# Token stage and routing stage merged into one block, with the tile order of the token stage rearranged

## The reference, cut to what matters

```python
x = L0_attn_x                                   # (4, 1024, 256): 4096 tokens of 256
x = layernorm(x + attention(x, kernel, WO))     # 16 heads of 64
probs = softmax(x @ gate_W)                     # 8 experts
topk_w, topk_idx = top_k(probs, 2)              # and topk_w normalized
out = 0.5 * gelu(x @ shared_W + shared_b)
for e in range(8):
    out = out + combine[:, e] * (gelu(x @ W1[e] + b1[e]) @ W2[e] + b2[e])
x = layernorm(x + layernorm(out) * gamma + beta)
```

## Time and profile before

| | us |
|---|---|
| median of 3 runs | 1883.01 (1877.25 to 1883.25) |
| the profiled execution, its own time | 1879.8 |
| its span | 1878.0 |
| TensorE busy | 1757.6 (94%) |
| VectorE busy | 1385.4 (74%) |
| ScalarE busy | 1046.4 (56%) |
| GpSimd busy | 353.7 (19%) |

### The profile page before, as it was taken

How to read it: one execution, slowest core, us unless ns; L and a number is a source line. 1 busy time by engine, 2 the same in 40 slices (tenths; PEclk the granted TensorE clock), 3 DMA queues, 4 the chain that set the end, 5 groups by cost and what they waited for, 6 DMA issues and landing times. The chain is left out here.

```text
span 1878.0 us, 31867 instructions
## 1 busy us (share of the span) xinstructions
PE 1757.6 (94%) x10909; PEld 1193.3 (64%) x10909; DVE 1385.4 (74%) x2213; ACT 1046.4 (56%) x1554; POOL 353.7 (19%) x399
## 2 busy tenths in 40 slices
PE   6999999999999999999999997987659999999986
PEld 5555555555555555555555553877549999999982
DVE  5888888888888888888888887555566655566647
ACT  5555555565555555555655654544455544455537
POOL 1000000000000000000000000011127766666654
PEclk9999999999999999999999998998879999999998
DMA  5011111111111111311111112444123333233335
GB/s 173 29 46 35 35 46 35 35 41 40 34 35 45 36 35 40 127 34 40 40 35 40 40 35 86 146 157 157 55 91 90 88 80 77 59 87 89 87 49 178
DMA packets 80198, 127.09 MB, mean 68 GB/s; under 512 B 12753, under 2 KB 46737, under 8 KB 77777
## 3 DMA queue, kind: packets, MB, share of 16 engines
q1 hardware_dynamic: 61808, 98.27, 15.6%
q0 software_dynamic: 18272, 27.31, 7.3%
HBM read 86.72 MB, written 38.83 MB: 67 GB/s over the span
## 5 line engine op out<-in xcount | busy, mean ns | idle before, releaser
L450 ACT ACTIVATE a_e<-banks 128x1024 f32<-128x1024 f32 x512 | 490.4, 1026 | 334.9 <-PE banks L346 334.9
L559 DVE TENSOR_TENSOR a_esum<-a_esum,a_e 128x1024 f32<-128x1024 f32 x384 | 470.4, 1225 | 80.5 <-ACT a_e L450 52.9
L360 PE MATMUL banks<-a_e,a_v 128*64 128x512 f32 x2048 | 481.6, 602 | 0.0
L360 PEld LDWEIGHTS banks<-a_e,a_v 128*64 128x64 f32 x2048 | 130.0, 136 | 251.2 <-issue 227.6
L346 PE MATMUL banks<-a_qh,a_kh 64*128 64x512 f32 x1024 | 222.8, 432 | 5.3 <-issue 5.3
L63 POOL MEMSET ident<- 128x128 f32 x1 | 0.2, 204 | 1139.9 <-POOLq L112 1139.9
L346 PEld LDWEIGHTS banks<-a_qh,a_kh 64*128 64x128 f32 x1024 | 96.2, 184 | 173.4 <-issue 107.9
L346 PE MATMUL banks<-a_qh,a_kl 64*128 64x512 f32 x1024 | 202.4, 391 | 0.0
L1790 ACT ACTIVATE e_g<-banks,e_b1c 128x256 f32<-128x256 f32 x280 | 114.9, 471 | 154.1 <-PE banks L1737 152.9
L346 PE MATMUL banks<-a_ql,a_kh 64*128 64x512 f32 x1024 | 200.2, 388 | 0.0
L1750 PE MATMUL banks<-e_w2h,e_hh 128*128 128x256 f32 x560 | 162.3, 290 | 4.5 <-issue 1.9
(11 more groups left out here) (232 smaller groups left out, 3294.4 us busy)
## 6 DMA issues: line engine op xcount, KB each, us to landing
attn_out<-a_ot SPq DMA_DIRECT2D x64, 256.0 KB, 2.0
a_inv<-inv_rows SPq DMA_DIRECT2D x126, 128.0 KB, 2.9
a_w<-w_qkv SPq DMA_DIRECT2D x32, 256.0 KB, 3.1
raw<-attn_out SPq DMA_DIRECT2D x4, 2048.0 KB, 8.8
t_ot<-attn_out SPq DMA_DIRECT2D x4, 2048.0 KB, 8.2
raw<-w_up SPq DMA_DIRECT2D x8, 1024.0 KB
raw<-w_down SPq DMA_DIRECT2D x8, 1024.0 KB
raw<-x_t SPq DMA_DIRECT2D x8, 512.0 KB, 9.3
```

Of the source, the lines that this page charges most:

```text
L360: mm = pe.matmul(o_acc[h * DH:(h + 1) * DH, :], v[quad % 2][:, n, head], e[(slot * ST + n) % NE][:, h * BANK:(h + 1) * BANK], start=n == 0 ...
L450: act.activation(e[t % NE], ring[n % RING], ACT.Exp, scale=SCALE).then_inc(e_ok, 1)
L559: dve.tensor_tensor(acc[:, :], acc[:, :], e[(slot * ST + n) % NE], ALU.add).then_inc(add_ok, 1)
```

## The change

The functions `tokens` and `routing` become one function with one block. Four things change in it.

1. The order of the token loop. `inverse` stands at the head of VectorE's step, ahead of `ot_low`. `gelu(n)` stands one step later on ScalarE (`gelus_after`). `branch` stands ahead of `turn` on TensorE. Tiles 24 to 31 are turned two to a step from step 29 on (`turn_at`). `top` is spread over two steps, `count` comes one step later, `rank` three steps after `top` in place of one, and `places` four in place of two.
2. The sort's parts are 8, 8, 12 and 4 tiles. The low digits of the first two parts are made on GpSimd, those of the others on VectorE, with one instruction for each of the 2 x 32 tile rows in place of one for many, and they carry the tile's number in place of a one. So the matmuls of `sort` need two kinds of columns, 128x160, in place of three, and `labelled` and ScalarE's share in it are gone. The reading of the result takes more steps, among them a reciprocal (mark, round). The last part's running sums are made on TensorE in place of GpSimd (`last_rank`, `totals`).
3. What `routing` waited for at the block's start is gone. The constants are made after the first tile in place of ahead of it. `b2all`, then the weights of the first expert, are loaded when their room in `raw` is free.
4. GpSimd gathers the first chunk's rows inside the block, as soon as their numbers are there. `up_l` is made in `experts`.

```diff
-    PARTS = [range(0, 8), range(8, 16), range(16, 24), range(24, 30), range(30, TT)]
+    PARTS = [range(0, 8), range(8, 16), range(16, TT - 4), range(TT - 4, TT)]
+    EARLY = {TT - 5: TT - 1}
...
-        turns = {}
...
+        turn_at = {n: n + 5 if n < TT - 8 else TT - 3 + (n - TT + 8) // 2 for n in range(TT)}
+        branch_step = {n: EARLY.get(n, turn_at[n + 1] if n + 1 < TT else TT) for n in range(TT)}
...
+        def gelus_after(t):
+            return [n for n in range(TT) if branch_step[n] + (n not in EARLY) == t]
...
+            def lows(p):                                        # GpSimd
+                gp.wait_ge(low_ok, p + 1)
+                for j in range(TOPK):
+                    for t in PARTS[p]:
+                        gp.tensor_scalar(low_hot[:, j, t, :], counting[:, :], low[:, j, t:t + 1], float(MARK + j * TT + t),
+                                         ALU.is_equal, ALU.mult).then_inc(lows_ok, 1)
...
+                for p in range(LAST):                           # GpSimd's loop
+                    if tops[p] + (p < LAST - 1) == t:
                         count(p)
+                    if p < LAST - 1 and tops[p] + 4 == t:
+                        lows(p)
...
+            gp.wait_ge(rows_out, 16 * len(GROUPS))
+            gp.wait_ge(numbers_ok, 1)
+            for a in range(CT):
+                gp.indirect_dma_start(out=xg[0][:, a, :], out_offset=None, in_=x2_rows,
+                                      in_offset=bass.IndirectOffsetOnAxis(ap=numbers[:, 0, 0, a:a + 1], axis=0))\
+                  .then_inc(xg_in[0], 16)
...
                 if t < TT:                                      # TensorE's loop
                     project(t)
+                for n in branched_after(t):
+                    if turn_at[n] < t:
+                        branch(n)
+                if t == TT:
+                    rank(LAST - 1)
                 for n in turned_after(t):
                     turn(n)
-                    if n:
-                        branch(n - 1)
...
+                for p in range(LAST - 1):
+                    if tops[p] + 3 == t:
                         rank(p)
+            last_rank()
+            totals()
...
-                for n in turned_after(t):                       # ScalarE's loop
+                for n in turned_after(t) if t < TT - 1 else ():
                     copy_turned(n)
-                    if n:
-                        gelu(n - 1)
+                for n in gelus_after(t):
+                    gelu(n)
...
             for t in range(TT + 1):                             # VectorE's loop
+                if t and ends_group(t - 1) is not None and t < TT:
+                    inverse(ends_group(t - 1))
                 if t + 2 < TT:
                     ot_low(t + 2)
+                for n in branched_before(t):
+                    biased(n)
+                    top(LAST - 1)
                 if t < TT:
                     add(t)
                     statistics(t)
-                if t and ends_group(t - 1) is not None:
-                    inverse(ends_group(t - 1))
...
+                if t == TT:
+                    inverse(ends_group(t - 1))
+                    places(LAST - 1)
+                    lows(LAST - 1)
...
+            ones_at(1)
...
+            lows(LAST)
             ones_at(2)
-            labelled(2)
+            ones_at(3)
+            ones_at(4)
```

More of the change, by code:

```diff
@@ new lines, in tokens @@
+        ends = [sb(f"r_ends{u}", [P, 2 * E]) for u in range(2)]
+        taken[0] = 2 * KD * HID + E * D
+        on_base = over(CH * E).rearrange("p (n e) -> p n e", e=E)
+        mark, own_row, tile_of, beyond, less, weight_row, target = (
+            over(PT).rearrange("p (a b) -> p a b", b=CT) for _ in range(7))
+        w_t = over(P)[0:CH, :]
+        w_all, place_base, at_tile = (over(CH) for _ in range(3))
+        assert taken[0] <= PAIRS * D + KD * (D + E) + PAIRS * HALF * P + HALF * D
@@ L1004, in rank, with last_rank @@
                 pe.matmul(out, ones[:, :], flat(cum, p), start=False, stop=True).then_inc(rank_done, 1)
+            def last_rank():
+                pe.wait_ge(hot_ok, LAST + 1)
+                start, n = PARTS[LAST][0], len(PARTS[LAST])
+                pe.matmul(ranks(LAST), before[:, :], flat(chosen, LAST), start=True, stop=False)
+                for t in range(n):
+                    mm = pe.matmul(banks[6 + LAST % 2][:, (start + t) * E:TT * E], ones[:, :],
+                                   (cum[:, start, :] if t == 0 else chosen[:, start:TT - t, :]).rearrange(
+                                       "p a b -> p (a b)") if t else
+                                   cum[:, start, :].unsqueeze(1).to_broadcast([P, n, E]), start=False, stop=t == n - 1)
+                mm.then_inc(rank_done, 1)
@@ new lines, in totals, with sort @@
+            def totals():
+                pe.wait_ge(r_done, TT)
+                start = PARTS[LAST][0]
+                pe.matmul(banks[0][:, 0:E], ones[:, :], cum[:, start, :], start=True, stop=False)
+                for t in range(start, TT):
+                    mm = pe.matmul(banks[0][:, 0:E], ones[:, :], chosen[:, t, :], start=False, stop=t == TT - 1)
+                mm.then_inc(totals_ok, 1)
+            def sort(part):
+                pe.wait_ge(ones_ok, part + 1)
+                pe.wait_ge(own_ok, part + 1)
+                for n in range(SORTS[part].start, SORTS[part].stop):
+                    mm = pe.matmul(banks[2][:, 0:2 * PT], low_hot[:, n // TT, n % TT, :],
+                                   high_hot[:, n, :, :].rearrange("p a b -> p (a b)"), start=n == 0, stop=n == CH - 1)
+                return mm
@@ L1189, in _ @@
                     statistics(t)
[L1190 to L1197 removed]
+                if t == 0:
+                    constants()
@@ L1355, in _ @@
+            top(LAST)
+            dve.tensor_tensor(gap[:, :], best[:, 1, :], best[:, 0, :], ALU.subtract).then_inc(gap_ok, 1)
+            places(LAST)
             dve.wait_ge(totals_ok, 1)
@@ L1407, in _ @@
-            dve.wait_ge(up_h_ok, 1)
-            dve.tensor_tensor(up_l[:, :], up[:, :], up_h[:, :].bitcast(F32), ALU.subtract).then_inc(up_l_ok, 1)
+            found = [banks[2][:, n * PT:(n + 1) * PT].rearrange("p (a b) -> p a b", b=CT) for n in range(2)]
+            own_marked, marked = found
+            link(dve.tensor_scalar(mark[:, :, :], marked, 1.0, None, ALU.max))
+            dve.tensor_scalar(tile_of[:, :, :], marked, float(MARK), -float(MARK), ALU.max, ALU.add)
+            link(dve.reciprocal(mark[:, :, :], mark[:, :, :]))
```

402 lines of the change are left out of this document (166 added, 236 removed).

## The result

| | before | after |
|---|---|---|
| median of 4 runs each, us | 1882.9 | 1838.1 (1836.8 to 1838.3) |
| the profiled execution, its own time | 1879.8 | 1836.8 |
| its span | 1878.0 | 1835.0 |
| first projection | 1171.0 | 1168.8 |
| token loop, up to the last projection | 168.5 | 137.2 |

The ratio is 0.9769, 95% interval 0.9753 to 0.9784. First the windows of the changed kernel, cut at the same events as the earlier trace rows: the loop, the time up to the experts' bases, the rest up to the sort's result, the way to the experts.

What follows compares the result with a forecast made beforehand. Attention and experts keep TensorE busy, so the gain was sought in token loop waits and routing: 3.1 (start) + 36.7 (loop) + 9.3 (tail) = 49.1 us off 1879.8, 1830.7, stated as 1832 between two bases; range 1821 to 1852.

Steps and rivals of the forecast that it cites:

- Start, 3.1 us: Block start: `wol` no longer stands behind GpSimd's constants, 3.1 us saved, first projection at 1167.8.
- The ring: Token loop: ScalarE's `gelu` and VectorE's `biased` wait on each other without overlap; a later `gelu` opens it. Loop: -36.7 us.
- A plain group costs TensorE nothing: Token loop: a group followed has `copy_turned` needed 9.9 against 10.9 us, so its end adds no TensorE wait.
- 126.8 + 5 us: Token loop: 126.8 us without stalls, mostly steps of 3.98, plus 5 us of stalls, 131.8 against 168.5.
- The first rival: Token loop: group ends stay as they are, perhaps as tile t+2's DMA holds `ot_high`; 21 us in place of 5, 1847; 16%.
- `rank` finds its count ready: Token loop: three steps after `top`, `rank` no longer waits for GpSimd's count, which had cost 15.4 us in three waits.
- The 5 us for late moments: Token loop: `top` or `places` before a group's end delays moments 2.5 us; TensorE stands some 1.5, three or four times.
- The tail, 46.1 us: Last projection to first expert matmul: 46.1 us in place of 55.4, a gain of 9.3.
- the list: Behind the last projection: linked pieces from `top` to the first expert matmul, priced one by one, 46.1 us taken.
- The prediction's estimate from the Trainium skill: VectorE's 24 `lows`: `tensor_scalar` at half a `tensor_tensor`'s time per element, some 1.5 us less, kernel 1829.
- GpSimd keeps up: Token loop: GpSimd's one-hot rows are stored in time; the rival that it cannot had 8%, 5 us twice, 1841.
- its sign of below 0.8 us each: Token loop: sign to look for in the changed profile, GpSimd's L1002 rows below 0.8 us each.

Runs made afterwards that it cites:

- the control: The changed kernel run once more, unedited, beside later edits on another chip: 1840.0 us, ratio 0.9778 to the kernel before.
- a_loads: Changed kernel with a half's two loads apart, attention output asked for earlier, a semaphore for each: 1814.8 us, ratio 0.9705 to the kernel before.
- a_pool_twice: Changed kernel with GpSimd's low digits of tiles 0 to 15 made twice: 1860.8 us, ratio 0.9880 to the kernel before.
- b_gelu_inverse: Kernel before with only `gelu` one step later on ScalarE and `inverse` ahead of `ot_low` on VectorE: 1850.4 us, ratio 0.9902 to the kernel before.
- b_rank: Kernel before with only `rank` of the first two parts, and their `places` and `lows`, two steps later: 1861.1 us, ratio 0.9957.
- a_gelu_back: Changed kernel with `gelu` of tiles 0 to 24 back in the step of its `branch`: 1833.6 us, ratio 0.9818 to the kernel before.
- a_inverse_back: Changed kernel with `inverse` back behind `ot_low`, `add` and `statistics`: 1847.8 us, ratio 0.9804 to the kernel before.
- a_tail_order: Changed kernel with `lows` of tiles 16 to 27 moved on VectorE behind `biased` and `top` of the last tiles: 1836.7 us, ratio 0.9757.
- a_split: Changed kernel with loads apart, third `pre` buffer, and 24 `lows` rows shared between VectorE and GpSimd: 1826.8 us, ratio 0.9700 to the kernel before.

## Why the prediction was right, and where it missed

- **The total.** 1838 lies in the range and 6 above 1832. On the profiled executions the change gave 43.0 us (1879.8 to 1836.8) against a sum of 49.1: 31.3 in the loop (36.7 forecast), 8.5 in the tail (9.3), 2.2 at the start (3.1) and 1.0 in the experts (0).
- **Start, 3.1 us.** TensorE's wait ahead of the loop fell from 11.9 to 8.8 us, 3.1 as summed. The first projection came at 1168.75 in place of 1167.8, because the end of attention moves by more than that: over the runs of the changed code it lay between 1167.8 and 1171.1.
- **The ring.** Right, and shown three ways: opening it in the kernel before (with `inverse`'s place), closing it again in the changed kernel, and the waits of ScalarE. Taking out `gelu`'s shift cost 8 to 12 us of the loop, taking out `inverse`'s place 4.5 to 8.
- **"A plain group costs TensorE nothing"** is the step that failed, with the loop's 126.8 + 5 us that rest on it. The hand-followed group had `ot_high` ready to run at its place. It had not. A half's loads are asked for only when `add` is done with the last tile of the half that had the same buffer, and `ot_high` needs them two steps later: 8 us at 3.98 each, where the landing takes 11 to 13. In the kernel before, steps of 5.3 us on average and a landing of some 10 us hid all but 2.8 us of it. The first rival named the DMA of tile t+2, and priced it with the group ends, not as a term of the sum. The loop came out 5.4 us over the sum (137.2 against 131.8); with the loads apart it is 6.4 to 10 us shorter, 130.8 and 131.6 us.
- **"`rank` finds its count ready"**: 2.0 us of waits remained, and went with the loads.
- **The 5 us for late moments** were too many. With the loads apart TensorE's waits for `copy_turned` are 1.6 us in all, and none is for `normalize`. The loop still exceeds the stall-free 126.8 by 4 to 5 us, so the total of 131.8 would have been met by it, but in part for other reasons: 1.5 us stood at the last steps, where `biased` waits for `pre`. With the third buffer that wait is gone and the loop is 1.2 us over; the rest of the difference is within what one loop differs from run to run.
- **The tail, 46.1 us.** 46.9 in the first profile, 48.1 in the control. The agreement is in part luck. The sort's result came 35.0 us behind the last projection where the list adds up to 36.1, in a run with the sort's last matmuls at full speed, and from there to the first expert matmul it took 11.9 us where the list has 9.9. `lows` of 12 tiles took 4.79 us (0.20 each, 0.19 was taken):

```profile
1313.57 4.79 DVE L1307 TENSOR_SCALAR t_low_hot<-t_counting,t_low 128x128 bf16<-128x128 f32 x24
```

The prediction's estimate from the Trainium skill, "VectorE: DVE Perf Modes", perf-mode tier table, put these 24 at some 3.1 us. The row does not agree with that estimate. It says little of the table itself, which is about the time per element: an instruction of 8 columns in the same tail takes 0.17 us (L1367), so little of the 0.20 hangs on the columns, and the rows of this kernel were the better guide.
- **GpSimd keeps up**, as the forecast had it, but with less to spare than its sign of below 0.8 us each. Most rows took 0.71 us, single ones up to 1.76, and the mean of the first part is 0.87 (minimum, median and maximum in ns):

```profile
L1002 POOL TENSOR_SCALAR t_low_hot<-t_counting,t_low x32: 705/714/1762, 1244.8 to 1292.5; 128x128 bf16<-128x128 f32 x32
```

- **The clock** of the loop came back from 0.90 to 0.99, as forecast. The experts kept their time (482.1 of 483.1).

## What to carry to other kernels

When a loop is made shorter, go through everything in it that is asked for a fixed number of steps ahead: its lead in microseconds shrinks with the step, and a transfer that was hidden by two slow steps is not hidden by two fast ones. A wait for a transfer holds what stands behind it in the engine's list, so ask for it as early as its own buffer allows, and give two loads with different last readers two semaphores (here both were done at once, and were worth 6 to 10 us). And where two engines hand work to each other within one step, move one of the two by a step before shortening either.

## What the runs showed of the hardware

- 512 KB of rows asked for 0.4 us behind a load of 2 MB landed after a median of 11.4 to 12.5 us in the changed kernel; asked for 5 to 8 us later, as in a_loads, after 3.9 to 5.1 us, while the 2 MB took 8 to 10 us in both.
- A GpSimd instruction of 128x128 took 0.71 us in most cases, and at times 1.3 to 1.8 us; in a row of 24 beside VectorE's busy tail the mean was 1.00. In the first part of a_pool_twice six of 32 took over 1.3 us, and each of them overlaps one of the six `ot_low` in that stretch, which read two tiles from SBUF. The `chosen` of 64 columns took 1.23 us again beside `ot_low`, and 0.33 us in a_pool_twice, where no `ot_low` ran beside it. The Trainium skill, "GPSIMD Engine Reference", section "Key points", says that GpSimd contends with VectorE instructions that have two SBUF inputs. These rows agree with it; in that stretch each `ot_low` lengthened one of the 32, and the rest kept their 0.71 us.
- In the set of b_gelu_inverse, b_rank, a_gelu_back and a_loads the experts took 465 to 472 us, in all other profiles 479 to 484, while a step of the token loop without waits took 3.98 us in a_loads as in the first profile. In a_loads TensorE has 2096 matmuls in the first 247.1 us of the experts, in the first profile 2030, at the same clock of 0.99. Why is open.
- The same 33 matmuls at the sort's end took 2.5 us at a granted clock of 1.00 in the first profile, a_loads and a_inverse_back, and 3.9 us at 0.61 to 0.63 in the control, a_tail_order, a_gelu_back and a_split. The engine had been idle for 1.5 to 1.9 us ahead of them in all seven. What decides between the two, these runs don't show.
- Still open is what of a_split's 2 to 3 us in the tail belongs to which of its two moves.
